# Start of a grouped-attention stage: six first pieces and four turned pairs in banks of their own, value tiles behind the first scores

## The chip, the cores and the metric

One core of a Trainium2 chip runs the whole program: a decoder of two layers on four sequences of 256 rows of 256 columns. The metric is the time on the device of one execution, in microseconds (us), as the median of the runs of a kernel.

## What is computed

The change lies in the attention of the last layer's block. Cut to what matters:

```python
h = rmsnorm(x, ln1_w)                       # B=4, S=256, H=256
q = rope((h @ Wq).reshape(B, S, 32, 128))   # 32 query heads of 128
k = rope((h @ Wk).reshape(B, S, 4, 128))    # 4 key heads, each for 8 query heads
v = (h @ Wv).reshape(B, S, 4, 128)
scores = einsum('bqhd,bkhd->bhqk', q, repeat(k, 8)) / sqrt(128)
scores = where(causal, scores, -1e9)
o = einsum('bhqk,bkhd->bqhd', softmax(scores), repeat(v, 8))
x = x + o.reshape(B, S, 32 * 128) @ Wo
```

Here x is the layer-normalised stream, which is normalised a second time for h. Everything is float32. Matmuls are made of three passes: each operand is split into a high part (fp32r) and a low part (the rest), and high by high, high by low and low by high are summed.

## The kernel before

The program is a row of six stages with a barrier between them. The stage in question is `stage_attention_1`; an expert stage (`stage_moe_1`) follows it. Each engine has a list of instructions that is written out in the order of the code, and waits on counting semaphores (`wait_ge`). Nothing else sets the order.

The stage has 64 steps (N = NP * B: 16 pairs of query heads by 4 sequences). A step takes one pair of heads of one sequence: `scores` (12 matmuls into a bank that already holds the causal mask), `maxima` on VectorE, `exps` on ScalarE, `normalise_probs` on GpSimd, `turn_probs` two steps later, `values` three steps later, `project` four steps later, and `residual`, which adds the result to the stream. Beside that each step makes one **piece**: a query or key head for two sequences, as six matmuls of 512 columns (`piece`). VectorE multiplies it by cosine and sine in three operations (`rotate`, L2229 to L2232, into prod), GpSimd adds the two products (`add`, L1889, into raw), ScalarE takes the high part (`high`, L2106) and GpSimd the low part (`low`, L1894).

PSUM has eight banks of 512 float32 columns: LONG (0 and 1) and SHORT (2) for scores, TURN0 and TURN1 (3, 4) for turned probabilities, PIECE (5), AV (6), OUT (7). ScalarE writes the causal mask into LONG and SHORT before scores are added to them (`mask_long` L2111, `mask_short` L2117).

Ahead of step 0 there is a start of the stage's own. VectorE normalises eight tiles (`normalise`), TensorE turns them in four pairs (`turn`, L1951) in banks 0 and 1 by turns, so that pair 2 waits until the low part of pair 0 is taken out of bank 0 (`h_high` L2094 on ScalarE, `h_low` L2216 on VectorE). Then come the six first pieces (key head 0 and the two query heads of pair 0, in two halves each), in banks PIECE and SHORT by turns, each waiting until the rotation of the piece two before it has read its bank. The eight value tiles (`values_of`, six matmuls of 512 columns each, `v_high` L2099, `v_low` L2261) stand between the pieces. TensorE waits for the last of them (s_vl) before step 0, and ScalarE for the same before the first mask. VectorE makes the residual's eight tiles (`residual_of`, L2209) before the first maxima.

```python
            for b in range(B):
                residual_of(b)
            e.wait_ge(s_res, NT)
            for n in range(N + PO + 1):
```

Of the kernel before, what the change touches and what calls it, by code (L numbers as in the profile page):

```python
# [13 lines left out]
B = 4  # L14
# [1742 lines left out]
def stage_attention_1(core, d):  # L1757
# [28 lines left out]
    with ExitStack() as ctx:  # L1786
# [45 lines left out]
        @block.sync  # L1832
        def _(e):
            e.dma_start(ln1[:], d["ln1"]).then_inc(s_ln1, 16)
            e.dma_start(wk[:], d["a1_wk"]).then_inc(s_wk, 16)
            e.dma_start(wv[:], d["a1_wv"]).then_inc(s_wv, 16)
            e.dma_start(wq[:, 0], d["a1_wq"][0:2].rearrange("h p k c -> p h k c")).then_inc(s_wq[0], 16)
            e.dma_start(rot[:], d["rot"]).then_inc(s_rot, 16)
            e.dma_start(seed[:], d["a1_seed"]).then_inc(s_seed, 16)
            e.dma_start(wo[:, 0], d["a1_wo"][:, 0:2, :]).then_inc(s_wo[0], 16)  # L1840
            e.dma_start(wq[:, 1], d["a1_wq"][2:4].rearrange("h p k c -> p h k c")).then_inc(s_wq[1], 16)
            e.dma_start(wo[:, 1], d["a1_wo"][:, 2:4, :]).then_inc(s_wo[1], 16)
            for p in range(2, NP + 2):
                if p < NP:
                    e.wait_ge(s_pc, number["q", p - 2, 1, 1] + 1)
                    e.dma_start(wq[:, p % 2], d["a1_wq"][2 * p:2 * p + 2].rearrange("h p k c -> p h k c"))\
                        .then_inc(s_wq[p % 2], 16)
                r = p - 2
                if r >= 2:
                    e.wait_ge(s_out, B * (r - 1))  # L1850
                    e.dma_start(wo[:, r % 2], d["a1_wo"][:, 2 * r:2 * r + 2, :]).then_inc(s_wo[r % 2], 16)

        V_BANKS = (TURN0, TURN1, AV, OUT, *LONG, AV, OUT)

        def bank_of(i):

            return ps[:, SHORT if i < FIRST and i % 2 else PIECE, :]

# [46 lines left out]
        def _(e):  # L1905
# [3 lines left out]
            const_low(e, 1)  # L1909
            for i in range(FIRST):  # L1910
                add(e, i)
                low(e, i)
            wo_low(e, 0)
            wq_low(e, 1)
            for n in range(N + 1):
# [15 lines left out]
        def _(e):  # L1931
# [12 lines left out]
            def turn(b):  # L1944
                e.wait_ge(s_n, 2 * b + 2)
                if b >= 2:
                    e.wait_ge(s_hl, b - 1)
                bank = ps[:, b % 2, :].rearrange("p (k t) -> p k t", k=KD)
                for j in range(2):
# [5 lines left out]
            def piece(i):  # L1955
                what = pieces[i]
                half = what[2]
                if i >= FIRST:
                    e.wait_ge(s_rp, 3 * i)
                elif i >= 2:  # L1960
                    e.wait_ge(s_rp, 3 * (i - 1))
                if i < FIRST:
# [40 lines left out]
            def turn_probs(s):  # L2003
                e.wait_ge(s_nrm, 2 * s + 2)
                if s >= 1:
                    e.wait_ge(s_tl, 2 * s)
# [10 lines left out]
            def values(s):  # L2017
                p, b = s // B, s % B
                g = p // 4
                e.wait_ge(s_tl, 2 * s + 2)  # L2020
                if s >= 1:
                    e.wait_ge(s_ol, s)
# [29 lines left out]
            piece(3)  # L2052
            piece(4)
            for t in range(4, 6):
                values_of(t)
            piece(5)
            for t in range(6, 8):
                values_of(t)
# [17 lines left out]
        def _(e):  # L2076
# [13 lines left out]
            def h_high(b):  # L2090
                e.wait_ge(s_tn, b + 1)
                bank = ps[:, b % 2, :].rearrange("p (k t) -> p k t", k=KD)
# [61 lines left out]
            wq_high(0)  # L2154
            h_high(2)
            const_high(1)
            h_high(3)
# [7 lines left out]
            for t in range(4, 6):  # L2165
                v_high(t)
            high(5)
            for t in range(6, 8):
                v_high(t)
            e.wait_ge(s_seed, 16)  # L2170
            e.wait_ge(s_vl, NT)
            mask_long(0)
            e.wait_ge(s_rp, 3 * FIRST)
            mask_short(0)
            wo_high(0)
            wq_high(1)
            for n in range(N + LV):
                for i in of_step.get(n - 1, ()):
                    high(i)
                if n + 1 < N:  # L2180
                    mask_long(n + 1)
                if n < N:
                    exps(n)
                if 0 <= n - LT < N:
                    turned_high(n - LT)
                if n + 1 < N:
                    mask_short(n + 1)
# [9 lines left out]
        def _(e):  # L2197
# [14 lines left out]
            def h_low(b):  # L2212
                e.wait_ge(s_hh, b + 1)
                bank = ps[:, b % 2, :].rearrange("p (k t) -> p k t", k=KD)
                for k in range(KD):
# [53 lines left out]
            def residual(s):  # L2269
                b = s % B  # L2270
                e.wait_ge(s_out, s + 1)
                e.tensor_tensor(res[:, 2 * b:2 * b + 2, :], res[:, 2 * b:2 * b + 2, :],  # L2272
                                ps[:, OUT, :].rearrange("p (t n) -> p t n", t=2), ALU.add).then_inc(s_add, 1)
# [11 lines left out]
            const_low(e, 0)  # L2285
            h_low(1)
            h_low(2)
# [9 lines left out]
            for t in range(4, 6):  # L2297
                v_low(t)
            rotate(5)
            for t in range(6, 8):  # L2300
                v_low(t)
            for b in range(B):
                residual_of(b)
            e.wait_ge(s_res, NT)
            for n in range(N + PO + 1):
# [4 lines left out]
                if n < N:  # L2310
                    maxima(n)
                if 0 <= n - PO - 1 < N:
# [458 lines left out]
```

## Time and profile before

| | us |
|---|---|
| median of 3 runs (1447.58 to 1452.32) | 1449.29 |
| the profiled execution | 1451.44 |
| its span | 1449.7 |
| TensorE (PE) busy in the span | 1267.7 (87%) |
| VectorE (DVE) | 958.6 (66%) |
| ScalarE (ACT) | 748.3 (52%) |
| GpSimd (POOL) | 632.2 (44%) |
| mean granted clock of TensorE | 0.938 of 2.4 GHz |

The busy shares are means over six stages. The grouped-attention stage begins at about 692 us of the span and ends at about 1140; the chain of work that ended last is, behind it, nearly all TensorE in the expert stage. What bounds the stage's start is read from the stretches of that start, not from the shares above.

### The profile page before, as it was taken

Reading aid. Unit: us, or ns where it says so; the run is one execution under the profiler, and the core shown is the slowest. Engines: PE = TensorE matmul, PEld = TensorE weight load, DVE = VectorE, ACT = ScalarE, POOL = GpSimd, SP = SyncE. Lnnn points to the kernel's source line nnn. Section 1 sums busy time; section 2 is a strip of 40 time slices with the busy share of each in tenths; the row PEclk is TensorE's granted clock in tenths of the full one; section 3 lists DMA queues with packets and bytes.
Section 4 is the critical chain, followed back from the end, with each engine's and each line's share of the span. In section 5 each row is a group of like instructions: output and inputs, shape, how many; then the busy total and the mean of one; then the engine's idle time right before and its main releaser. Section 6 shows DMA issues by size and latency. Waiting matters only on the chain. (4 is left out here: it accounts for less than half of the span.)

```text
span 1449.7 us, 23461 instructions
## 1 busy us (share of the span) xinstructions
PE 1267.7 (87%) x8399; PEld 995.9 (69%) x8399; DVE 958.6 (66%) x1761; ACT 748.3 (52%) x1685; POOL 632.2 (44%) x617
## 2 busy tenths in 40 slices
PE   5788668989889668888769999999999899999998
PEld 4665444744468444543558898898899778888887
DVE  5773773658745678883568898898898743344343
ACT  2555113346442136666357777786887444444442
POOL 5210101001044541200457887877886545555553
PEclk8999787989999869998879999999999899999999
DMA  2000400030000100000200010000100123323321
GB/s 75 1 2 2 117 3 0 1 111 0 0 1 1 40 1 2 2 2 1 82 8 16 16 30 16 30 16 16 30 16 16 46 98 109 119 101 111 117 101 55
DMA packets 28803, 54.80 MB, mean 38 GB/s; under 512 B 6170, under 2 KB 15706, under 8 KB 28612
## 3 DMA queue, kind: packets, MB, share of 16 engines
q1 hardware_dynamic: 28708, 53.55, 11.5%
q8 instruction: 58, 0.95, 0.3%
q14 instruction: 37, 0.30, 0.1%
HBM read 52.22 MB, written 1.21 MB: 37 GB/s over the span
## 5 line engine op out<-in xcount | busy, mean ns | idle before, releaser
L2618 DVE TENSOR_TENSOR e_act<-e_gated,ps 128x512 f32<-128x512 f32 x66 | 45.4, 688 | 157.5 <-POOL e_gated L2419 157.5
L1889 POOL TENSOR_TENSOR a_raw<-a_prod 128x512 f32<-128x512 f32 x72 | 93.0, 1291 | 65.6 <-DVE a_prod L2232 64.5
L2131 ACT ACTIVATE a_prob<-ps,a_nmax 128x128 f32<-128x128 f32 (+1 forms) x256 | 103.3, 413 | 7.0 <-DVE a_nmax L2239 6.2
L2419 POOL TENSOR_TENSOR e_gated<-e_gate,e_wb 128x512 f32<-128x512 f32 x66 | 85.1, 1291 | 49.4 <-ACT e_gate L2540 43.8
L2410 POOL TENSOR_TENSOR e_we_low<-e_we,e_we_high 128x768 fp32r<-128x768 f32 x33 | 61.3, 1856 | 86.9 <-ACT e_we_high L2545 86.2
L1665 DVE SCALAR_TENSOR_TENSOR m_acc<-ps,m_conv_w,m_acc 128x1020 f32<-128x1020 f32 (+2 forms) x60 | 76.1, 1275 | 28.5 <-ACT m_acc L1581 27.1
L1939 PE MATMUL ps<-a_k_high,a_q_high 128*128 128x128 f32 (+1 forms) x256 | 73.8, 288 | 20.0 <-ACT ps L2117 20.0
L1415 PE MATMUL ps<-m_ln_T,m_win 128*128 128x512 f32 x192 | 86.4, 604 | 3.6 <-DMA m_win<-in_m_winT 3.0
L612 DVE TENSOR_REDUCE x_nmax<-ps 128x2 bf16<-128x512 f32 x128 | 82.3, 689 | 10.0 <-PE ps L383 10.0
L2540 ACT ACTIVATE e_gate<-ps 128x512 f32<-128x512 f32 x66 | 39.3, 597 | 91.3 <-PE ps L2473 91.2
L518 ACT ACTIVATE x_probT<-ps 128x512 f32<-128x512 f32 x128 | 69.3, 595 | 31.0 <-PE ps L399 29.6
L1894 POOL TENSOR_TENSOR a_q_low<-a_raw,a_q_high 128x512 fp32r<-128x512 f32 x64 | 82.4, 1288 | 3.0 <-ACT a_q_high L2106 3.0
L95 POOL TENSOR_SCALAR row_var<-row_moments 128x2 f32<-128x2 f32 x20 | 4.9, 246 | 167.9 <-DVE row_moments L76 167.9
L2106 ACT ACTIVATE a_q_high<-a_raw 128x512 fp32r<-128x512 f32 x64 | 40.6, 635 | 71.3 <-POOL a_raw L1889 71.3
L2550 ACT ACTIVATE e_act_high<-e_act 128x512 fp32r<-128x512 f32 x66 | 41.5, 630 | 61.0 <-DVE e_act L2618 61.0
L1939 PE MATMUL ps<-a_k_low,a_q_high 128*128 128x128 f32 (+1 forms) x256 | 72.5, 283 | 0.0
L1939 PE MATMUL ps<-a_wo_high,a_o_high 128*128 128x256 f32 x256 | 71.7, 280 | 0.9 <-DVE res L2272 0.9
L2491 PE MATMUL ps<-e_we_high,e_act_low 128*128 128x256 f32 x256 | 72.4, 283 | 0.0
L2491 PE MATMUL ps<-e_we_low,e_act_high 128*128 128x256 f32 x256 | 72.4, 283 | 0.0
L1939 PE MATMUL ps<-a_k_high,a_q_low 128*128 128x128 f32 (+1 forms) x256 | 72.3, 282 | 0.0
L2491 PE MATMUL ps<-e_we_high,e_act_high 128*128 128x256 f32 x256 | 72.3, 282 | 0.0
L1939 PE MATMUL ps<-a_wo_high,a_o_low 128*128 128x256 f32 x256 | 71.7, 280 | 0.0
(429 smaller groups left out, 4302.1 us busy)
## 6 DMA issues: line engine op xcount, KB each, us to landing
e_wb<-token_weights SPq DMA_DIRECT2D x32, 512.0 KB, 4.0
e_we<-in_experts SPq DMA_DIRECT2D x33, 384.0 KB, 3.1
a_wq<-in_a_wq SPq DMA_DIRECT2D x16, 256.0 KB, 2.8
a_wo<-in_a_wo SPq DMA_DIRECT2D x16, 256.0 KB, 2.7
m_win<-in_m_winT SPq DMA_DIRECT2D x2, 1024.0 KB, 8.8
nf_pickU<-in_nf_pickU SPq DMA_DIRECT2D x1, 1152.0 KB
nf_raw<-in_ffn_w SPq DMA_DIRECT2D x3, 352.0 KB
x<-in_x SPq DMA_DIRECT2D x4, 256.0 KB, 6.1
```

Source lines behind the costliest of these rows:

```text
L518: e.activation(probT[:, n % 8, :], shifted_bank(n), ACT.Exp).then_inc(s_ex, 1)
L612: e.tensor_reduce(nmax[:, c % 2, :, col], score_bank(n).rearrange("p (j k) -> p j k", j=2), AX.X, ALU.max, negate=True).then_inc(s_nm, 1)
L1415: mm = e.matmul(ps[:, 2 * (i % RING) + half, :], win[:, k, at:at + P], lnT[:, k, half * BANK:(half + 1) * BANK], start=(k == 0), stop=(k = ...
L1665: e.scalar_tensor_tensor(sums[:, :, back:S], chan[:, :, 0:S - back], conv_w[:, c, TAPS - 1 - back:TAPS - back], sums[:, :, back:S], ALU.mu ...
L1889: e.tensor_tensor(raw[:, i % 2, :], prod[:, i % 2, 0, :], prod[:, i % 2, 1, :], ALU.add).then_inc(s_raw, 1)
L1894: e.tensor_tensor(low_part, raw[:, i % 2, :], high_part.bitcast(F32), ALU.subtract).then_inc(s_xl, 1)
L1939: mm = e.matmul(out, a, b, start=first and at == 0, stop=last and at == n - 1, skip_group_check=seeded and not first)
L2131: ins = e.activation(prob[:, n % PR, at + j * w:at + (j + 1) * w], bank[:, j * w:(j + 1) * w], ACT.Exp, bias=nmax[:, n % 2, j, t:t + 1], a ...
L2410: e.tensor_tensor(weL[:, slot, :], we[:, slot, :], weH[:, slot, :].bitcast(F32), ALU.subtract).then_inc(s_wl, 1)
L2419: e.tensor_tensor(gated[:, half, :], gate[:, half, :], wb[:, s % SLOTS, half * BANK:(half + 1) * BANK], ALU.mult).then_inc(s_gw, 1)
L2491: mm = e.matmul(ps[:, 4 + t // 2, t % 2 * D:(t % 2 + 1) * D], a[:, s % 2, t * P:(t + 1) * P], dw(w, s % SLOTS), start=(first and t % 2 == ...
L2618: e.tensor_tensor(act[:, half, :], gated[:, half, :], ps[:, 2 * half + 1, :], ALU.mult).then_inc(s_act, 1)
```

## The change

- The four turned pairs get a bank each (TURN0, TURN1, AV, OUT), and the six first pieces too (LONG twice, SHORT, PIECE, AV, OUT). The waits for a bank between them go.
- TensorE does the four turns, the six pieces, then step 0. Value tiles 0 to 2 stand behind the scores of step 0, 3 to 5 behind those of step 1, 6 and 7 behind those of step 2; `v_high` and `v_low` go with them.
- The low parts of the first three pieces go from GpSimd to VectorE, each one rotation behind. The rotation of the sixth piece stands behind the maxima of step 0.
- The masks of step 0 are written between the first high parts; in steps 0 to 3 the next short mask comes right behind the exps, and the high parts of new pieces behind it.
- The residual's tiles are made in steps 2 to 5, one pair in each. The first query weights are loaded ahead of the value weights.

```diff
             e.dma_start(wk[:], d["a1_wk"]).then_inc(s_wk, 16)
+            e.dma_start(wq[:, 0], d["a1_wq"][0:2].rearrange("h p k c -> p h k c")).then_inc(s_wq[0], 16)
             e.dma_start(wv[:], d["a1_wv"]).then_inc(s_wv, 16)
-            e.dma_start(wq[:, 0], d["a1_wq"][0:2].rearrange("h p k c -> p h k c")).then_inc(s_wq[0], 16)
...
-        V_BANKS = (TURN0, TURN1, AV, OUT, *LONG, AV, OUT)
+        V_BANKS = (TURN0, TURN1, AV, OUT) * 2
+        VALUES_AT = {0: (0, 1, 2), 1: (3, 4, 5), 2: (6, 7)}
+        FIRST_BANKS = (*LONG, SHORT, PIECE, AV, OUT)
+        turn_bank = lambda b: ps[:, (TURN0, TURN1, AV, OUT)[b], :].rearrange("p (k t) -> p k t", k=KD)
 
         def bank_of(i):
 
-            return ps[:, SHORT if i < FIRST and i % 2 else PIECE, :]
+            return ps[:, FIRST_BANKS[i] if i < FIRST else PIECE, :]
...
-            for i in range(FIRST):
+            for i in range(3):
+                add(e, i)
+            wq_low(e, 1)
+            e.wait_ge(s_xl, 3)
+            for i in range(3, FIRST):
                 add(e, i)
                 low(e, i)
             wo_low(e, 0)
-            wq_low(e, 1)
...
             def turn(b):
                 e.wait_ge(s_n, 2 * b + 2)
-                if b >= 2:
-                    e.wait_ge(s_hl, b - 1)
...
-                if i >= FIRST:
+                if i == FIRST:
+                    e.wait_ge(s_rp, 3 * (FIRST_BANKS.index(PIECE) + 1))
+                if i > FIRST:
                     e.wait_ge(s_rp, 3 * i)
-                elif i >= 2:
-                    e.wait_ge(s_rp, 3 * (i - 1))
...
                 if t == 0:
                     e.wait_ge(s_wcl, 2)
-                if t >= 6:
+                    e.wait_ge(s_hl, B)
+                if t in (2, 3):
+                    e.wait_ge(s_rp, 3 * (t + 3))
+                if t >= 4:
                     e.wait_ge(s_vl, t - 3)
...
-            turn(0)
-            turn(1)
-            turn(2)
-            piece(0)
-            turn(3)
-            piece(1)
-            piece(2)
-            for t in range(4):
-                values_of(t)
...
-            e.wait_ge(s_vl, NT)
+            for b in range(B):
+                turn(b)
+            for i in range(FIRST):
+                piece(i)
             for n in range(N + PO):
                 new = [*of_step.get(n, ())]
                 if n < N:
                     scores(n)
+                for t in VALUES_AT.get(n, ()):
+                    values_of(t)
...
+            e.wait_ge(s_seed, 16)
+            e.wait_ge(s_rp, 3)
+            mask_long(0)
             high(1)
+            wq_high(1)
             high(2)
-            for t in range(4):
-                v_high(t)
+            e.wait_ge(s_rp, 9)
+            mask_short(0)
             high(3)
             high(4)
...
-            e.wait_ge(s_vl, NT)
-            mask_long(0)
-            e.wait_ge(s_rp, 3 * FIRST)
-            mask_short(0)
-            wo_high(0)
-            wq_high(1)
             for n in range(N + LV):
-                for i in of_step.get(n - 1, ()):
-                    high(i)
+                if n > 3:
+                    for i in of_step.get(n - 1, ()):
+                        high(i)
...
                 if n < N:
                     exps(n)
+                if n <= 3:
+                    mask_short(n + 1)
+                for t in VALUES_AT.get(n, ()):
+                    v_high(t)
+                if n == 0:
+                    high(FIRST - 1)
+                    wo_high(0)
+                if n <= 3:
+                    for i in of_step.get(n - 1, ()):
+                        high(i)
...
             rotate(0)
-            h_low(3)
             rotate(1)
+            low(e, 0)
             rotate(2)
-            for t in range(4):
-                v_low(t)
+            low(e, 1)
             rotate(3)
+            low(e, 2)
             rotate(4)
...
-            for b in range(B):
-                residual_of(b)
-            e.wait_ge(s_res, NT)
...
                 if n < N:
                     maxima(n)
+                if n == 0:
+                    rotate(FIRST - 1)
+                if 0 <= n - 2 < B:
+                    residual_of(n - 2)
                 if 0 <= n - PO - 1 < N:
                     residual(n - PO - 1)
                 new = [*of_step.get(n, ())]
                 for i in new[:1]:
                     rotate(i)
+                for t in VALUES_AT.get(n, ()):
+                    v_low(t)
```

GpSimd's list at the start of the stage, before (a_raw is `add`, a_k_low and a_q_low are `low`):

```order
L1877 TENSOR_TENSOR a_wq_low<-a_wq,a_wq_high 128x512
L1873 TENSOR_TENSOR a_wv_low<-a_prob,a_wv_high 128x1024
L1889 TENSOR_TENSOR a_raw<-a_prod 128x512
L1894 TENSOR_TENSOR a_k_low<-a_raw,a_k_high 128x512
L1889 TENSOR_TENSOR a_raw<-a_prod 128x512
L1894 TENSOR_TENSOR a_q_low<-a_raw,a_q_high 128x512
```

and now:

```order
L1880 TENSOR_TENSOR a_wq_low<-a_wq,a_wq_high 128x512
L1876 TENSOR_TENSOR a_wv_low<-a_prob,a_wv_high 128x1024
L1892 TENSOR_TENSOR a_raw<-a_prod 128x512 x3
L1880 TENSOR_TENSOR a_wq_low<-a_wq,a_wq_high 128x512
L1892 TENSOR_TENSOR a_raw<-a_prod 128x512
L1897 TENSOR_TENSOR a_k_low<-a_raw,a_k_high 128x512
```

Three adds follow each other, their low parts are gone from this list, and the low part of the next query weights stands behind them.

VectorE's list around the first maxima, before (a_prod is `rotate`, a_v_low `v_low`, res `residual_of`, a_nmax `maxima`):

```order
L2229 TENSOR_TENSOR a_prod<-ps,a_rot 128x512
L2230 TENSOR_TENSOR a_prod<-ps,a_rot 64x512
L2232 TENSOR_TENSOR a_prod<-ps,a_rot 64x512
L2261 TENSOR_TENSOR a_v_low<-ps,a_v_high 128x512 x2
L2209 TENSOR_SCALAR res<-x,row_moments,row_rstd 128x256 x8
L2239 TENSOR_REDUCE a_nmax<-ps 128x2
L2242 TENSOR_REDUCE a_nmax<-ps 128x2
```

and now, from the third low part on:

```order
L1897 TENSOR_TENSOR a_q_low<-a_raw,a_q_high 128x512
L2234 TENSOR_TENSOR a_prod<-ps,a_rot 128x512
L2235 TENSOR_TENSOR a_prod<-ps,a_rot 64x512
L2237 TENSOR_TENSOR a_prod<-ps,a_rot 64x512
L2244 TENSOR_REDUCE a_nmax<-ps 128x2
L2247 TENSOR_REDUCE a_nmax<-ps 128x2
```

Low parts of pieces have come in between the rotations; the values' low parts and the residual's eight tiles no longer stand ahead of the first maxima.

ScalarE's list around the first exps, before (ps from a_seed is a mask, a_prob the exps):

```order
L2099 ACTIVATE a_v_high<-ps 128x512 x2
L2111 ACTIVATE ps<-a_seed 128x512
L2117 ACTIVATE ps<-a_seed 128x256
L2088 ACTIVATE a_wo_high<-a_wo 128x512
L2084 ACTIVATE a_wq_high<-a_wq 128x512
L2111 ACTIVATE ps<-a_seed 128x512
L2131 ACTIVATE a_prob,a_rsum<-ps,a_nmax 128x128 x2
```

and now, as a piece of the difference:

```order
+L2117 ACTIVATE ps<-a_seed 128x256
 L2106 ACTIVATE a_k_high<-a_raw 128x512
 L2106 ACTIVATE a_q_high<-a_raw 128x512
+L2111 ACTIVATE ps<-a_seed 128x512
+L2131 ACTIVATE a_prob,a_rsum<-ps,a_nmax 128x128 x2
+L2131 ACTIVATE a_prob,a_rsum<-ps,a_nmax 128x256 x2
+L2117 ACTIVATE ps<-a_seed 128x256
+L2099 ACTIVATE a_v_high<-ps 128x512 x3
```

The first exps stand behind the high parts of pieces 3 and 4, the short mask of step 1 right behind the exps, and the values' high parts behind that.

## Rows read from the trace of the kernel before

**Rows 1.** Windows: busy us (instructions) by engine, granted clock, DMA share, GB/s.
```profile
723.00:733.00 10.00, 0.33 (x2) 0.21 (x2) 5.88 (x12) 4.43 (x9) 4.15 (x4) 0.73 0.00 0
733.00:758.30 25.30, 19.70 (x90) 16.36 (x91) 17.06 (x30) 14.82 (x51) 16.22 (x16) 0.77 0.04 10
758.30:770.20 11.90, 11.89 (x85) 11.00 (x86) 10.79 (x21) 9.73 (x30) 8.98 (x9) 1.00 0.01 3
770.20:830.00 59.80, 56.32 (x384) 50.66 (x383) 51.84 (x95) 42.81 (x132) 47.33 (x45) 1.00 0.06 19
```

**Rows 2.** Timeline of TensorE: start, us, instruction; first score matmul of steps 0-6.
```profile
732.82 0.45 PE L1939 MATMUL ps<-a_k_high,a_q_high 128*128 128x128 f32 x1 [9.67 <-ACT ps L2117]
...
738.87 0.30 PE L1939 MATMUL ps<-a_k_high,a_q_high 128*128 128x128 f32 x1 [0.27 <-ACT ps L2117]
...
745.34 0.45 PE L1939 MATMUL ps<-a_k_high,a_q_high 128*128 128x128 f32 x1 [2.87 <-ACT ps L2117]
...
752.99 0.30 PE L1939 MATMUL ps<-a_k_high,a_q_high 128*128 128x128 f32 x1 [1.10 <-ACT ps L2117]
...
758.31 0.30 PE L1939 MATMUL ps<-a_k_high,a_q_high 128*128 128x128 f32 x1 [0.59 <-ACT ps L2117]
...
764.29 0.22 PE L1939 MATMUL ps<-a_k_high,a_q_high 128*128 128x128 f32 x1
...
770.19 0.22 PE L1939 MATMUL ps<-a_k_high,a_q_high 128*128 128x128 f32 x1
```

**Rows 3.** Timeline of TensorE: the first piece, and matmuls of 512 columns following each other.
```profile
699.92 0.79 PE L1939 MATMUL ps<-a_h_high,a_wk_high 128*128 128x512 f32 x1 [0.74 <-DVE a_h_low L2216]
...
708.46 0.39 PE L1939 MATMUL ps<-a_wv_high,a_h_low 128*128 128x512 f32 x1
708.69 0.39 PE L1939 MATMUL ps<-a_wv_high,a_h_high 128*128 128x512 f32 x1
...
736.74 0.63 PE L1939 MATMUL ps<-a_h_low,a_wq_high 128*128 128x512 f32 x1
737.17 0.63 PE L1939 MATMUL ps<-a_h_high,a_wq_low 128*128 128x512 f32 x1
...
759.77 0.40 PE L1939 MATMUL ps<-a_h_high,a_wq_high 128*128 128x512 f32 x1
```

**Rows 4.** Timeline of ScalarE, VectorE and GpSimd around the first piece.
```profile
698.29 0.63 ACT L2084 ACTIVATE a_wq_high<-a_wq 128x512 fp32r<-128x512 f32 x1 [0.21 <-DMA a_wq<-in_a_wq]
...
702.95 0.69 DVE L2229 TENSOR_TENSOR a_prod<-ps,a_rot 128x512 f32<-128x512 f32 x1 [1.99 <-PE ps L1939]
...
705.16 1.30 POOL L1889 TENSOR_TENSOR a_raw<-a_prod 128x512 f32<-128x512 f32 x1 [1.64 <-DVE a_prod L2232]
...
706.50 0.63 ACT L2106 ACTIVATE a_k_high<-a_raw 128x512 fp32r<-128x512 f32 x1 [1.93 <-POOL a_raw L1889]
```

**Rows 5.** Three lines of the code: count, min/median/max ns, first and last start.
```profile
L2574 DVE TENSOR_TENSOR e_t_low<-e_tT,e_t_high x4: 678/1216/5036, 1149.4 to 1157.2; 128x512 fp32r<-128x512 f32 x4
...
L2424 POOL TENSOR_TENSOR x<-x,res x1: 5002/5002/5002, 1151.7 to 1151.7; 128x2048 f32<-128x2048 f32 x1
...
L2209 DVE TENSOR_SCALAR res<-x,row_moments,row_rstd x8: 407/412/1375, 731.6 to 734.8; 128x256 f32<-128x256 f32 x8
```

**Rows 6.** Timeline of VectorE: value tiles, residual tiles, and the maxima of step 1.
```profile
714.20 2.49 DVE L2261 TENSOR_TENSOR a_v_low<-ps,a_v_high 128x512 fp32r<-128x512 f32 x4 [4.01 <-ACT a_v_high L2099]
...
731.59 4.59 DVE L2209 TENSOR_SCALAR res<-x,row_moments,row_rstd 128x256 f32<-128x256 f32 x8
...
740.89 0.39 DVE L2239 TENSOR_REDUCE a_nmax<-ps 128x2 f32<-128x256 f32 x1
741.21 0.68 DVE L2242 TENSOR_REDUCE a_nmax<-ps 128x2 f32<-128x512 f32 x1
```

**Rows 7.** Timeline of ScalarE in step 1: long mask, then (behind the exps) short mask.
```profile
742.71 0.58 ACT L2111 ACTIVATE ps<-a_seed 128x512 f32<-128x512 bf16 x1
...
744.80 0.39 ACT L2117 ACTIVATE ps<-a_seed 128x256 f32<-128x256 bf16 x1
```

More of the change, by code:

```diff
@@ L1945, in turn @@
                 e.wait_ge(s_n, 2 * b + 2)
-                if b >= 2:
-                    e.wait_ge(s_hl, b - 1)
-                bank = ps[:, b % 2, :].rearrange("p (k t) -> p k t", k=KD)
+                bank = turn_bank(b)
                 for j in range(2):
@@ L2004, in turn_probs @@
                 e.wait_ge(s_nrm, 2 * s + 2)
+                if s == 0:
+                    e.wait_ge(s_vl, 6)
                 if s >= 1:
@@ L2020, in values @@
                 e.wait_ge(s_tl, 2 * s + 2)
+                if s == 0:
+                    e.wait_ge(s_vl, NT)
                 if s >= 1:
@@ L2041, in project @@
                 mm.then_inc(s_out, 1)
-            turn(0)
-            turn(1)
-            turn(2)
-            piece(0)
-            turn(3)
-            piece(1)
-            piece(2)
-            for t in range(4):
-                values_of(t)
[L2052 to L2058, printed above, removed]
-            e.wait_ge(s_vl, NT)
+            for b in range(B):
+                turn(b)
+            for i in range(FIRST):
+                piece(i)
             for n in range(N + PO):
@@ L2091, in h_high @@
                 e.wait_ge(s_tn, b + 1)
-                bank = ps[:, b % 2, :].rearrange("p (k t) -> p k t", k=KD)
+                bank = turn_bank(b)
                 for k in range(KD):
@@ L2155, in _ @@
             h_high(2)
+            h_high(3)
             const_high(1)
-            h_high(3)
             high(0)
+            e.wait_ge(s_seed, 16)
+            e.wait_ge(s_rp, 3)
+            mask_long(0)
             high(1)
+            wq_high(1)
             high(2)
-            for t in range(4):
-                v_high(t)
+            e.wait_ge(s_rp, 9)
+            mask_short(0)
             high(3)
             high(4)
[L2165 to L2170, printed above, removed]
-            e.wait_ge(s_vl, NT)
-            mask_long(0)
-            e.wait_ge(s_rp, 3 * FIRST)
-            mask_short(0)
-            wo_high(0)
-            wq_high(1)
-            for n in range(N + LV):
-                for i in of_step.get(n - 1, ()):
-                    high(i)
+            for n in range(N + LV):
+                if n > 3:
+                    for i in of_step.get(n - 1, ()):
+                        high(i)
+                if n == 0:
+                    e.wait_ge(s_rp, 6)
                 if n + 1 < N:
@@ L2183, in _ @@
                     exps(n)
+                if n <= 3:
[8 more added lines that the diff above has]
+                        high(i)
                 if 0 <= n - LT < N:
                     turned_high(n - LT)
-                if n + 1 < N:
+                if 3 < n < N - 1:
                     mask_short(n + 1)
@@ L2213, in h_low @@
                 e.wait_ge(s_hh, b + 1)
-                bank = ps[:, b % 2, :].rearrange("p (k t) -> p k t", k=KD)
+                bank = turn_bank(b)
                 for k in range(KD):
@@ L2271, in residual @@
                 e.wait_ge(s_out, s + 1)
+                if s < B:
+                    e.wait_ge(s_res, 2 * b + 2)
                 e.tensor_tensor(res[:, 2 * b:2 * b + 2, :], res[:, 2 * b:2 * b + 2, :],
@@ L2285, in _ @@
             const_low(e, 0)
-            h_low(1)
-            h_low(2)
+            for b in range(1, B):
+                h_low(b)
             e.wait_ge(s_rot, 16)
             rotate(0)
-            h_low(3)
             rotate(1)
+            low(e, 0)
             rotate(2)
-            for t in range(4):
-                v_low(t)
+            low(e, 1)
             rotate(3)
+            low(e, 2)
             rotate(4)
[L2297 to L2301, printed above, removed]
-            for b in range(B):
-                residual_of(b)
-            e.wait_ge(s_res, NT)
             for n in range(N + PO + 1):
@@ L2311, in _ @@
                     maxima(n)
+                if n == 0:
+                    rotate(FIRST - 1)
+                if 0 <= n - 2 < B:
+                    residual_of(n - 2)
                 if 0 <= n - PO - 1 < N:
```

## The prediction

> **What bounds the kernel now.** I read the windows view first, cut at the places where TensorE's work changes character in the grouped-attention stage [rows 1]. From 758.30 us on TensorE is busy in 11.89 of 11.90 us, and in 56.32 of the 59.80 us after that: the steps of the stage run at TensorE's pace, some 6 us each. Before that they do not. From 723 to 733 us TensorE works 0.33 us in 10, and from 733 to 758.30 it is granted 0.77 of its clock. So the time that this change can reach lies between 700 and about 770 us, and whatever is won there moves all that follows to an earlier place, since what follows does not wait for a transfer.
>
> Next the timeline, for the first score matmul of steps 0 to 6 [rows 2]. They start at 732.82, 738.87, 745.34, 752.99, 758.31, 764.29 and 770.19 us. Step 0 began after TensorE had sat idle for 9.67 us, released by ScalarE's short mask; step 2 after 2.87 us. The reader is to see that step 0, and not the matmuls, is late. ScalarE writes the masks behind all eight value tiles, these wait for VectorE, and VectorE does them between the six first rotations and before the eight tiles of the residual.
>
> A matmul of 512 columns follows the next one by 0.23 us at the full clock (2.4 GHz) and by 0.43 us at the lower one (1.2 GHz) [rows 3]. Six of them, a piece or a value tile, are thus 1.38 or 2.56 us. The 12 score matmuls of step 4 took 1.46 us (758.31 to the piece at 759.77) [rows 2, 3]; at the lower clock I put them at 2.5, a little under twice that, an estimate.
>
> **Up to the first scores, part by part.** The first piece starts at 699.92 us [rows 3]; what it waits for (the low part of pair 1, the key weights) keeps its place. With a bank for every turned pair, pairs 2 and 3 are turned earlier, beside the wait for that low part: nothing on the path. The transfer of wq, now ahead of wv, can give ScalarE back the 0.21 us that it waited for wq [rows 4], or nothing; the value weights land that much later, and their turn on ScalarE is later too, behind pair 3. I take zero.
>
> The six pieces no longer wait for a rotation to empty a bank. Two of them run in part at the lower clock, and all are done by about 710 us. VectorE sets the pace instead. A rotation takes from 702.95 us to 705.16, when GpSimd starts adding its products [rows 4]: 2.15 us of VectorE and the signal. VectorE now does rotation 0, rotation 1, low 0, rotation 2, low 1, rotation 3, low 2 and then scores may start. A low part from two SBUF tiles is new on VectorE here; the same operation takes 678 ns at its shortest elsewhere, with 0.62 us from one pass to the next [rows 5, 6]. Four rotations are 8.6, three lows 1.95: 702.95 + 10.55 = 713.5 us. The add (1.30 us), the high part (0.63) and the hand-over of a piece end 2.0 us behind its rotation [rows 4], so they hide beside the next rotation; the short mask follows the high part of piece 2, at 712.5.
>
> One thing does not hide: while GpSimd runs an operation, VectorE's operation on two SBUF tiles stands still. In the expert stage that same low part took up to 5036 ns, in the very stretch in which GpSimd's 128x2048 addition took 5002 ns from 1151.7 on [rows 5]. Here every low starts when GpSimd is given an add. Where VectorE is first, GpSimd is what waits, 0.6 us; then low 2 meets GpSimd's low part of the next query weights and ends 0.4 us later, which I take. Where GpSimd is always first, each of two lows waits an operation of 1.3 us: 2.6 us more, my other end. Step 0 starts at 714.0 us where it was 732.82: **18.8 us earlier**.
>
> The Trainium skill ("SBUF — State Buffer", section "Who interferes with whom") says this as a rule against the change: an instruction of VectorE with two SBUF inputs and a GpSimd instruction that reads SBUF take turns, the second waiting for the whole of the first. By that rule the sum is the same, and its bad end is the rival on the port below; the trace agrees, with its 5036 ns.
>
> **What comes back in steps 0 to 6.** The value tiles are not gone: 11 us of TensorE (8 x 1.38) and their passes move into steps 0 to 2, the residual (4.59 us for eight tiles [rows 6]) into steps 2 to 5, rotation 5 into step 0. I follow the path from step to step.
>
> Step 0: TensorE was idle for some 4 us before it, and behind the idle 2.87 us in the rows it ran at the lower clock; so scores 2.5 us, first value tile 2.56, two more 2.76, piece 1.4: step 1 at 723.3. ScalarE must have the short mask back by then. Its exps stand behind high 4, which waits for two adds and a low on GpSimd (3 x 1.3 us) and a high part (0.7) from low 2 on: 718.6, high 0.6; long mask and exps 2.1 (742.71 to 744.80 [rows 7]); short mask 0.4: 721.7, in time.
>
> Step 1: scores, three value tiles, a piece, 7 us: step 2 at 730.2. VectorE's rotation of piece 6, three low parts of values (0.62 each [rows 6]) and maxima (0.39 and 0.68 us [rows 6]) with exps and mask behind them end at the same time.
>
> From here on VectorE, then exps and mask, end last. Step 2: rotation 2.15, three value lows 1.9, inverse and maxima 1.15, from 730.3 on, then 1.4 for the rest of exps and mask: step 3 at 737.0. Step 3: the first residual pair 1.15, rotation 2.15, two value lows 1.3, two passes on the turned probabilities 1.05, maxima 1.15: step 4 at 743.7. Step 4: residual pair, rotation, turned probabilities, a low of the output 0.65, maxima, and on ScalarE the turned high parts (0.85) between exps and mask: step 5 at 751.0. Step 5: the same, and project 1 waits for the first addition to the residual (0.65) and takes 1.4: step 6 at 757.9. Before, it was 770.19: **12.3 us earlier**. VectorE has next to no slack in these steps; that is where 6.5 of the 18.8 us go.
>
> The residual pairs are priced at their mean of the old place, 1.15 us. One tile is 412 ns in the middle and 1375 ns where GpSimd was at work [rows 5]. In the new place GpSimd is always at work: it normalises probabilities from the inverse on, which stands 1 us ahead of the pair. I take 1.5 us for a pair, between 0.7 (two free tiles) and 2.7 (two blocked): 4 x 0.35 = 1.4 us off. Sum: 12.3 - 1.4 = **11 us**, rounded.
>
> The profiled execution took 1451.44 us, its span 1449.7; the sum makes it 1440.4. The median of the runs shown, 1449.29, lies 2.15 below that execution, so I forecast **1438.3 us**. The measurement tells about 0.3% (4.35 us) from no change: faster means below 1444.9, slower above 1453.6.
>
> **The rivals.**
> *The clock stays up and the port is free.* The wait ahead of step 0 is some 4 us, not 9.67; if the clock holds through it, scores and first value tile lose no time, but step 1 then waits for ScalarE's short mask at 721.7: 1.6 us. With residual pairs at 0.7 another 3.2 us. 11 + 4.8: 1433.5 us. Against it: the clock did fall behind 2.87 us [rows 2].
>
> *The port goes GpSimd's way every time.* 2.6 us ahead of step 0, and 4 x (2.7 - 1.5) = 4.8 us in the residual pairs: 11 - 7.4 = 3.6, 1445.7 us, no change by the bound. For it stand the 5036 and 1375 ns [rows 5]; against it, that VectorE reaches low 0 and low 1 straight from the rotation whose end GpSimd has to be told of.
>
> *Half the clock through steps 0 to 6.* Slower than before. From scores 0 to scores 6 TensorE has some 37 us of work at full clock (6 scores 8.7, 8 value tiles 11, 6 pieces 8.4, four turns 2.8, three value products 3.3, two projections 2.8); the forecast lets it take 44. If the waits between its blocks keep the clock at the lower level, as it was granted 0.73 and 0.77 from 723 to 758 us [rows 1], the work takes 74 and step 6 starts at 788, 18 us later than before: 1467 us. It decides against the change once some 24 us of that work, beyond what I have at half clock, run so. Against it: after step 0 no wait in my path is over 1 us, and the value tiles fill the gaps that the old steps 0 to 2 had.
>
> **How the numbers follow.** Forecast 0.67: the order of the engines is written out, and every term has its row, but the chain has four engines in it. Clock up and port free 0.16. Port against it 0.12. Half clock 0.05. Faster by over 0.3%: 0.67 + 0.16 = 0.83. Within 0.3%: 0.12. Slower: 0.05. The forecast's own terms (lows 0 to 2.6, pairs 0.7 to 2.7, the clock 1.6) make it 1434 to 1443; the range reaches down to the first rival and up to near the second, **1432 to 1445 us**, and leaves out the half clock and the end of the port case.
>
> **What the new profile would show.** The first score matmul near 714 us after an idle of 3 to 5 us, that of step 6 near 758. Three k_low and q_low on VectorE of about 0.69 us, or 1.3 to 2 where blocked. Residual tiles of VectorE in pairs, one of each pair well over 412 ns. TensorE at 0.5 of its clock for some 5 us from 714 on, then at 1.0. From about 760 us on the same pace as before. I would be wrong if step 0 started after 718, if step 4 came later than 748, if the clock fell again in steps 1 to 5, or if steps 7 to 63 took longer than they did.

## The result, and the profile after

The changed kernel takes 1440.30 us (median of 6 runs, 1434.53 to 1442.71), and the kernel before, on the same chip, 1450.76 (6 runs, 1446.52 to 1454.79). The ratio is 0.9928, with a 95% interval of 0.9901 to 0.9956: **faster by 10.5 us**. The forecast was 11 us, to 1438.3 us, in a range of 1432 to 1445.

| | before | changed |
|---|---|---|
| the profiled execution | 1451.44 | 1438.6 |
| its span | 1449.7 | 1436.6 |
| first normalise of the stage | 692.23 | 689.37 |
| first piece | 699.92 | 697.06 |
| mean granted clock | 0.938 | 0.942 |

The spans differ by 13.1 us. Of these, 2.86 lie ahead of the stage, where the program is the same, and are no part of the change; all steps below are therefore counted from the first matmul of the first piece. The timeline of TensorE in the changed kernel (start in us, duration, instruction; in brackets the idle time before it and what ended it) has in this order the first piece, the first score matmuls of steps 0 to 4, and the first projection:

```profile
697.06 0.79 PE L1945 MATMUL ps<-a_h_high,a_wk_high 128*128 128x512 f32 x1 [1.59 <-DVE a_h_low L2221]
...
710.84 0.33 PE L1945 MATMUL ps<-a_k_high,a_q_high 128*128 128x128 f32 x1 [3.51 <-DVE a_q_low L1897]
...
719.36 0.22 PE L1945 MATMUL ps<-a_k_high,a_q_high 128*128 128x128 f32 x1
...
726.67 0.22 PE L1945 MATMUL ps<-a_k_high,a_q_high 128*128 128x128 f32 x1
...
733.55 0.30 PE L1945 MATMUL ps<-a_k_high,a_q_high 128*128 128x128 f32 x1
...
740.11 0.30 PE L1945 MATMUL ps<-a_k_high,a_q_high 128*128 128x128 f32 x1 [0.60 <-ACT ps L2117]
...
754.09 0.35 PE L1945 MATMUL ps<-a_wo_high,a_o_high 128*128 128x256 f32 x1 [2.18 <-DVE res L2279]
```

These answer to [rows 2]. The reader is to see that the 9.67 us of idle time ahead of step 0 are 3.51, ended by the last of VectorE's new low parts, and that there is a new wait of 2.18 us for VectorE ahead of the first projection. From the first piece on, in us:

| step | before | forecast | changed | gain | second profile of the changed kernel |
|---|---|---|---|---|---|
| 0 | 32.90 | 14.1 | 13.78 | 19.1 | 13.86 |
| 1 | 38.95 | 23.4 | 22.30 | 16.7 | 22.39 |
| 2 | 45.42 | 30.3 | 29.61 | 15.8 | 29.72 |
| 3 | 53.07 | 37.1 | 36.49 | 16.6 | 36.60 |
| 4 | 58.39 | 43.8 | 43.05 | 15.3 | 43.16 |
| 5 | 64.37 | 51.1 | 50.05 | 14.3 | 50.17 |
| 6 | 70.27 | 58.0 | 58.53 | 11.7 | 58.66 |
| 7 | 77.56 | | 67.37 | 10.2 | 65.95 |
| 10 | 97.75 | | 87.57 | 10.2 | 86.16 |

(The forecast column is without its 1.4 us for the residual, which no step was given.) From step 7 to step 63 the gain stays between 10.14 and 10.24 us; the steady step is 5.90 us in both. The last column, from the run further down, shows that step 6 to 7 differs between executions of the same kernel.

The windows of the changed kernel, columns as in [rows 1], show at what the first steps run:

```profile
700.00:714.00 14.00, 10.49 (x44) 8.73 (x44) 13.22 (x20) 3.81 (x7) 9.11 (x7) 0.87 0.07 21
714.00:722.00 8.00, 8.00 (x41) 6.65 (x40) 4.51 (x8) 6.05 (x17) 5.39 (x6) 0.96 0.00 0
722.00:730.00 8.00, 7.61 (x39) 6.02 (x38) 5.63 (x11) 5.01 (x15) 5.78 (x6) 1.00 0.00 0
730.00:738.00 8.00, 7.12 (x40) 5.59 (x40) 7.91 (x17) 4.79 (x16) 5.25 (x6) 1.00 0.00 0
738.00:746.00 8.00, 7.40 (x51) 6.49 (x49) 7.91 (x14) 6.59 (x24) 7.59 (x8) 1.00 0.10 35
746.00:758.00 12.00, 9.17 (x58) 8.34 (x58) 11.81 (x21) 6.92 (x21) 5.96 (x7) 0.90 0.00 1
```

VectorE (third count) is busy 13.22 of the 14 us around the start of step 0 (710.84), and from its first rotation at 700.09 to the end of the last low part at 710.79 it has no wait: it sets the pace there, as forecast. From 714 to 730 (the rest of step 0, step 1 and half of step 2) TensorE is busy 15.61 of 16 us and VectorE is free for 5.9. From 730 to 758 it is the other way round: VectorE 27.63 of 28 us, TensorE with gaps. VectorE's own lines tell why:

```profile
704.42 0.69 DVE L1897 TENSOR_TENSOR a_k_low<-a_raw,a_k_high 128x512 fp32r<-128x512 f32 x1
...
707.19 0.69 DVE L1897 TENSOR_TENSOR a_q_low<-a_raw,a_q_high 128x512 fp32r<-128x512 f32 x1
...
709.96 0.83 DVE L1897 TENSOR_TENSOR a_q_low<-a_raw,a_q_high 128x512 fp32r<-128x512 f32 x1
...
719.55 0.69 DVE L2234 TENSOR_TENSOR a_prod<-ps,a_rot 128x512 f32<-128x512 f32 x1 [3.34 <-PE ps L1945]
...
726.88 0.69 DVE L2234 TENSOR_TENSOR a_prod<-ps,a_rot 128x512 f32<-128x512 f32 x1 [2.28 <-PE ps L1945]
...
731.83 1.34 DVE L2214 TENSOR_SCALAR res<-x,row_moments,row_rstd 128x256 f32<-128x256 f32 x2
...
738.37 1.17 DVE L2214 TENSOR_SCALAR res<-x,row_moments,row_rstd 128x256 f32<-128x256 f32 x2
...
744.14 2.32 DVE L2214 TENSOR_SCALAR res<-x,row_moments,row_rstd 128x256 f32<-128x256 f32 x2
...
751.06 2.29 DVE L2214 TENSOR_SCALAR res<-x,row_moments,row_rstd 128x256 f32<-128x256 f32 x2
```

Three low parts (0.69, 0.69, 0.83 us), then waits of 3.34 and 2.28 us for pieces 6 and 7 in steps 0 and 1, and only behind these waits, where VectorE has no time left, the four residual pairs.

### The profile page after: what moved, and what is told of

It reads as the page before. It is cut to its first block and busy times, and to the rows that moved or that the text cites. A ratio compares the mean times of both kernels' runs of the same rounds, so it can differ in the third digit from the quotient of the medians.

```text
span 1436.6 us, 23466 instructions
## 1 busy us (share of the span) xinstructions
PE 1263.4 (88%) x8399; PEld 993.2 (69%) x8399; DVE 961.5 (67%) x1764; ACT 747.1 (52%) x1685; POOL 629.6 (44%) x614
## 3 DMA queue, kind: packets, MB, share of 16 engines
q1 hardware_dynamic: 28708, 53.55, 11.6%
```

## The experiments

Most were run once, and single times of one kernel differ by several us (the kernel before, on the second of these chips, 1442.10 to 1456.91). They are judged by their steps, counted from the first piece, and the time is given beside that of the kernel before on the same chip. Two parts of the change were never undone: the banks of the six pieces, and the place of the value tiles as a whole. What these are worth is read from the rows of the two kernels, not shown by an experiment.

**The residual pairs.** Theory: pairs in steps 2 to 5 stand on the path, and VectorE's waits in steps 0 and 1 could hold them. Rival: their place does not matter.

```diff
-                if 0 <= n - 2 < B:
-                    residual_of(n - 2)
+                if n < 2:
+                    residual_of(2 * n)
+                    residual_of(2 * n + 1)
```

> The residual's pairs are made in steps 0 and 1 (two pairs each, behind the maxima and ahead of the rotation), where VectorE waited 3.34 and 2.28 us for TensorE, instead of steps 2 to 5. Places are told from the first matmul of the first piece; the changed kernel has step 0 at 13.78, step 4 at 43.05, step 6 at 58.53, step 10 at 87.57 us. Theory (the pairs, stretched by GpSimd to 7.1 us, are what gives back the gain between steps 3 and 8): step 4 at 41, step 6 at 54, step 10 at 81 to 83 us. Rival (TensorE's value tiles and ScalarE's exps and masks set those steps, VectorE only follows): step 10 at 87 us or later.

Measured: 1430.83 us (before: 1444.95). The steps start at 13.79, 22.35, 29.67, 36.54, 42.86, 49.86, 55.85, and step 10 at 83.36: steps 0 to 5 stand within 0.2 us of the changed kernel, step 6 is 2.7 us earlier. VectorE's timeline, residual pairs 0 to 3 and the first operation of rotations 6, 7 and 8:

```profile
714.12 3.34 DVE L2214 TENSOR_SCALAR res<-x,row_moments,row_rstd 128x256 f32<-128x256 f32 x4
717.77 0.69 DVE L2234 TENSOR_TENSOR a_prod<-ps,a_rot 128x512 f32<-128x512 f32 x1 [0.30 <-PE ps L1945]
...
722.72 2.21 DVE L2214 TENSOR_SCALAR res<-x,row_moments,row_rstd 128x256 f32<-128x256 f32 x4
...
725.09 0.69 DVE L2234 TENSOR_TENSOR a_prod<-ps,a_rot 128x512 f32<-128x512 f32 x1 [0.16 <-PE ps L1945]
...
731.05 0.69 DVE L2234 TENSOR_TENSOR a_prod<-ps,a_rot 128x512 f32<-128x512 f32 x1 [0.92 <-PE ps L1945]
```

The waits of 3.34 and 2.28 us took in 5.55 us of residual. What follows: 2.7 us is the whole effect of the four pairs up to step 6, and 2.5 of it lie in step 5 (8.48 us in the changed kernel, 5.99 here). There pair 3 (2.29 us) stood right ahead of the addition that the first projection waits for, and the wait of 2.18 us is gone. Pairs 0 to 2 moved next to nothing by step 5: with pair 0 gone, VectorE waits 0.92 us for piece 8 instead, and from 735 to 745 us GpSimd is busy 10.00 of 10 us. The theory holds for step 5 only: it had step 4 at 41 and step 10 at 81 to 83 us. Of the 4.2 us at step 10, 1.4 are the clock in step 6 (below).

**All pairs ahead of the maxima**, where they stood before the change. Theory: the first steps lose 1 to 2 us, since the first exps waited for a high part anyway, and the later steps win 6. Rival: the place of the pairs does not matter, and the first steps lose 2 to 4 us.

```diff
             rotate(4)
+            for b in range(B):
+                residual_of(b)
...
-                if 0 <= n - 2 < B:
-                    residual_of(n - 2)
```

> All four residual pairs stand ahead of the first maxima, as in the kernel before; the rest as changed. Theory: the first maxima come some 4 us later, of which exps 0 hid 2 us (they waited for the high part of piece 4 until 716.0 us), so step 1 starts 1 to 2 us later than 22.30 us; steps 3 to 7 lose their pairs and win 6 us: step 10 at 83 to 84 us. Rival (the place of the residual doesn't matter, or it was right to move it): step 10 at 87.57 us plus the 2 to 4 us that the first steps lose, 89 to 91 us.

Measured: 1444.37 us (before: 1444.95); step 1 at 24.15 (+1.85), step 2 at 32.67 (+3.06), step 6 at 58.83, step 10 at 86.33. The eight tiles took 5.74 us in a row. The first maxima came 5.7 us later, the first exps 2.6. Behind a wait of 1.63 us for the short mask ahead of step 1 the clock fell (0.50 from 730 to 733 us), and step 1 to 2 took 8.52 us instead of 7.31. Step 1 is the theory's; step 10 lies between the two expectations, and against the changed kernel's second profile (86.16) it neither wins nor loses. Putting the pairs late was therefore no gain over putting them early; only the gaps of steps 0 and 1, used pair by pair, are.

**The first low parts back on GpSimd.** Theory: three GpSimd passes of 1.3 us beside three adds set step 0. Rival: a low part is as dear on VectorE, because of the port.

```diff
             for i in range(3):
                 add(e, i)
+                low(e, i)
             wq_low(e, 1)
-            e.wait_ge(s_xl, 3)
...
             rotate(1)
-            low(e, 0)
...
```

> The first three low parts are on GpSimd again, each behind its add; the rest as changed. Theory (moving them to VectorE took GpSimd's 3.3 us per piece off the path, and the port cost only what GpSimd waited): step 0 at 15 to 15.5 us instead of 13.78, step 10 at 87.5 to 89 us. Rival (the port makes a low part on VectorE as dear as on GpSimd): step 0 at 13.8 us or earlier, step 10 at 87 us or earlier.

Measured: 1438.48 us (before: 1444.95); step 0 at 15.12 (+1.34), step 1 at 24.91 (+2.61), step 10 at 88.67, which is 2.5 later than the second profile of the changed kernel. Step 0 to 1 took 9.79 us instead of 8.52: TensorE had waited 4.71 us and had half the clock until 718 us, 6 us into step 0, not some 3.7. The theory holds, and the move of the low parts is 1.3 of the 19.1 us at step 0.

**Value tiles ahead of step 0.** Theory: two value tiles fill the idle 3.51 us and keep the clock up in step 0, but steps 2 to 7 are set by VectorE and ScalarE. Rival: TensorE's lost time is carried through, and every step comes 2.3 to 2.8 us earlier.

```diff
             for i in range(FIRST):
                 piece(i)
+            values_of(0)
+            values_of(1)
...
                 for t in VALUES_AT.get(n, ()):
-                    values_of(t)
+                    if t > 1:
+                        values_of(t)
```

> TensorE makes value tiles 0 and 1 ahead of the scores of step 0, in the 3.51 us in which it was idle. Theory (VectorE and ScalarE set steps 2 to 7, the clock and TensorE only steps 0 and 1): no lower clock in step 0, step 1 up to 0.9 us earlier than 22.30 (the short mask is there 0.9 us ahead of it), steps 2 and 3 up to 2 us earlier, step 10 at 86 to 87.6 us. Rival (TensorE's lost time is carried through): every step from 1 on, and step 10, 2.3 to 2.8 us earlier, 85 us.

Measured: 1443.37 us (before: 1444.95); step 1 at 21.63 (0.67 earlier), but step 2 at 31.45 (1.84 later) and step 10 at 87.92. TensorE's timeline of this kernel, first score matmuls of steps 0 and 1:

```profile
715.00 0.33 PE L1945 MATMUL ps<-a_k_high,a_q_high 128*128 128x128 f32 x1 [0.81 <-DVE a_q_low L1897]
...
722.81 0.45 PE L1945 MATMUL ps<-a_k_high,a_q_high 128*128 128x128 f32 x1 [2.75 <-ACT ps L2120]
```

The windows of the same kernel around step 1 (granted clock third from the end):

```profile
719.00:723.00 4.00, 1.25 (x6) 0.78 (x5) 3.12 (x5) 3.37 (x12) 3.09 (x3) 0.90 0.00 0
723.00:727.00 4.00, 4.00 (x16) 3.71 (x17) 2.97 (x6) 3.93 (x13) 2.25 (x2) 0.50 0.00 0
```

The idle time ahead of step 0 is 0.81 us, but the work taken from step 0 left 2.75 us of waiting for the short mask ahead of step 1, and there the clock fell to 0.50. The idle time had only moved one step on. Neither expectation had this: step 1 is the theory's, but steps 2 and 3 came 1.84 us later, where the theory had them up to 2 us earlier, and step 10 lies beyond both. One tile ahead, on top of the first experiment, gave little:

> As the run with the residual in the idle time of steps 0 and 1, and TensorE makes one value tile, not two, ahead of the scores of step 0: 1.4 of its 3.15 us of idle are filled. Theory (the clock falls in the wait that is left, be it ahead of step 0 or of step 1, which waits for its short mask at about 21.4 us): if a wait of 2 us lets it fall, step 2 at 30 us or later and step 10 at 83.4 to 85; if it stays up, step 1 at 21.4, step 2 at 28.7, step 10 at 82.5 to 83.4 us.

Measured: 1435.43 us (before: 1448.38); step 1 at 21.71, step 10 at 83.08 against 83.36 in the first experiment: 0.3 us. TensorE waited 1.84 us ahead of step 0 and 0.43 ahead of step 1, and the clock fell behind the first (0.50 from 714.5 to 717.5 us). Even so step 2 came at 29.41 and step 10 at 83.08, earlier than expected for a clock that falls.

**ScalarE's order.** In steps 0 to 3 the change puts the next mask straight behind the exps, and the high parts of new pieces behind it. Theory: this order lets VectorE and TensorE of the next step go on. Rival: ScalarE has the time either way.

```diff
-                if n > 3:
-                    for i in of_step.get(n - 1, ()):
-                        high(i)
+                for i in of_step.get(n - 1, ()):
+                    high(i)
...
-                if n <= 3:
-                    mask_short(n + 1)
...
-                if 3 < n < N - 1:
+                if n < N - 1:
                     mask_short(n + 1)
```

> ScalarE's order in steps 0 to 3 is again that of the later steps: high parts of new pieces ahead of the exps, the next short mask behind the turned probabilities (and so behind the values' high parts too); the rest as changed. Places from the first matmul of the first piece, as before; the changed kernel has step 1 at 22.30, step 10 at 87.57 us. Theory (the short mask releases steps 1 to 3, so its place next to the exps is a part of the gain): the mask of step 1 moves behind three value high parts, a high part and the output weights, 2.6 us, of which 0.9 is slack: step 1 at 24 us, step 10 at 89 to 91 us. Rival (TensorE's own work sets steps 1 to 3): step 10 at 87.6 to 88 us.

Measured: 1443.97 us (before: 1448.38); step 1 at 24.24 (+1.9), step 3 at 41.37 (+4.9), step 5 at 55.08 and step 6 at 64.30, which are 4.9 and 5.6 later than in the changed kernel's second profile, and step 10 at 92.79. TensorE waited 1.54 us for the short mask ahead of step 1 and 1.81 ahead of step 3:

```profile
721.46 0.30 PE L1945 MATMUL ps<-a_k_high,a_q_high 128*128 128x128 f32 x1 [1.54 <-ACT ps L2117]
...
738.59 0.30 PE L1945 MATMUL ps<-a_k_high,a_q_high 128*128 128x128 f32 x1 [1.81 <-ACT ps L2117]
```

The two waits are 3.35 of the 4.9 us, and 1.2 came with the half clock behind the first (step 1 to 2 took 8.49 us, not 7.31). Whether the clock falls there each time is not shown by one profile. What is lost behind step 5 is not counted to the order: there the clock fell behind a wait of 2.17 us for VectorE that the changed kernel has too, and behind this wait a fall comes in one execution and not in another (below). The theory holds, with more than it asked for (step 10 at 89 to 91 us): at 4.9 us this order is the largest part of the change among those that were undone.

**Banks and transfers.** The two old turn banks with their wait, and wv ahead of wq. Theory: these parts only move work that nothing waits for. Rival: they set the first piece.

```diff
+            e.dma_start(wv[:], d["a1_wv"]).then_inc(s_wv, 16)
             e.dma_start(wq[:, 0], d["a1_wq"][0:2].rearrange("h p k c -> p h k c")).then_inc(s_wq[0], 16)
-            e.dma_start(wv[:], d["a1_wv"]).then_inc(s_wv, 16)
...
-        turn_bank = lambda b: ps[:, (TURN0, TURN1, AV, OUT)[b], :].rearrange("p (k t) -> p k t", k=KD)
+        turn_bank = lambda b: ps[:, (TURN0, TURN1)[b % 2], :].rearrange("p (k t) -> p k t", k=KD)
...
+                if b >= 2:
+                    e.wait_ge(s_hl, b - 1)
```

> The turned pairs share two banks again, with their wait, and the value weights are loaded ahead of the first query weights; the rest as changed. Theory (both lie beside other work): the first piece starts as late behind the stage's first instruction as in the changed kernel, step 0 at 13.8 us, step 10 at 87.6 us, all within 0.3 us. Rival (pair 3's late low part holds up pieces 3 to 5, which now follow each other without a wait): step 0 up to 1 us later, step 10 up to 1 us later.

Measured: 1437.03 us (before: 1448.38). From the first piece on the steps are those of the changed kernel up to step 6 (13.76 to 58.53), but the first piece itself comes 8.53 us behind the stage's first normalise (688.35 to 696.88), not 7.69. All four turns stand ahead of it on TensorE, and with two banks the last two wait for low parts. TensorE in this kernel:

```profile
694.23 1.09 PE L1957 MATMUL ps<-ident,a_normed 128*128 128x128 f32 x4 [2.93 <-DVE a_h_low L2223]
696.15 1.09 PE L1957 MATMUL ps<-ident,a_normed 128*128 128x128 f32 x4 [0.83 <-DVE a_h_low L2223]
```

Both waits are for low parts, not for a transfer. So the banks are worth 0.84 us to this order, and "the first piece starts as late" missed; step 10 at 86.05 missed 87.6 too, for the reason that follows. In this kernel step 6 to 7 took 7.29 us where the changed kernel's profile had 8.84, with the same wait of 2.18 us ahead of the projection. The windows of the changed kernel around that wait:

```profile
751.00:755.00 4.00, 1.82 (x14) 1.55 (x12) 3.97 (x6) 3.74 (x14) 2.20 (x2) 1.00 0.01 2
755.00:759.00 4.00, 4.00 (x22) 3.81 (x21) 3.60 (x9) 1.62 (x5) 2.48 (x3) 0.57 0.00 0
```

The second of these windows in the kernel with the old banks:

```profile
755.00:759.00 4.00, 4.00 (x30) 3.69 (x30) 3.94 (x10) 1.78 (x7) 2.66 (x3) 1.00 0.00 0
```

Whether that came with the banks or differs from execution to execution was asked of the changed kernel itself, unedited:

> The changed kernel as it is, a second time. In its first profiled execution the clock fell in step 6, behind 2.18 us of idle TensorE, and step 6 to 7 took 8.84 us; with the two old turn banks the same idle cost nothing (7.29 us). Theory (the fall differs from execution to execution of one kernel): either 8.8 or 7.3 us from step 6 to 7 here, all other steps from the first piece on within 0.1 us of the first profile, step 10 at 87.6 or at 86.0 us behind the first piece. Rival (four banks and the earlier wq bring it about): 8.8 us again. Theory and rival agree if 8.8 comes; 7.3 decides for the theory. Median 0.7% below the kernel before.

Measured: 1439.33 us (before: 1448.85; 6 runs, 1433.21 to 1442.88; ratio 0.9935, 0.9909 to 0.9961). Step 6 to 7 took 7.29 us, steps 0 to 6 stood within 0.13 us of the first profile, and step 10 came at 86.16. The wait ahead of the projection was 2.18 us again, at 753.07, and the windows around it show no fall:

```profile
750.00:754.00 4.00, 1.82 (x14) 1.55 (x13) 3.97 (x6) 3.72 (x14) 2.18 (x2) 1.00 0.01 2
754.00:758.00 4.00, 4.00 (x32) 3.69 (x30) 3.94 (x9) 1.62 (x5) 2.52 (x3) 1.00 0.00 0
```

The fall in step 6 is a matter of the execution, not of the banks. Without it the stage gives 11.6 us, with it 10.2.

**A better version.** In the first experiment step 5 is late by ScalarE: in step 4, whose order is already the later one, the mask and exps stand behind a high part that waits for GpSimd (TensorE waits 0.88 us for the short mask ahead of step 5). ScalarE's timeline there:

```profile
741.14 0.63 ACT L2106 ACTIVATE a_q_high<-a_raw 128x512 fp32r<-128x512 f32 x1 [1.41 <-POOL a_raw L1892]
741.68 0.58 ACT L2111 ACTIVATE ps<-a_seed 128x512 f32<-128x512 bf16 x1
```

So the first experiment was run with ScalarE's first order kept through step 4 (3 becomes 4 in its four conditions).

> As the run with the residual in the idle time of steps 0 and 1 (step 4 at 42.86, step 5 at 49.86, step 10 at 83.36 us), and ScalarE keeps the order of the first steps (exps, short mask, then high parts) in step 4 too. Theory (with the pairs gone, step 5 waits 0.88 us for the short mask, whose exps stood behind a high part that waited for GpSimd): step 5 0.9 us earlier, step 10 at 82.4 to 82.7 us, and a time of 1435 us or 1.0% below the kernel before. Rival (VectorE or GpSimd end last there too): step 10 at 83.3 us; then 0.9% below.

Measured: 1432.85 us (before: 1448.38; 7 runs; ratio 0.9902, 0.9864 to 0.9939); step 5 at 48.92 (0.94 earlier than in the first experiment), step 10 at 82.69, 0.67 earlier. The theory holds. It was measured once more beside the changed kernel:

> The version with residual pairs in steps 0 and 1 and ScalarE's first-steps order through step 4, a second time, beside the changed kernel on the same chip. Theory (the stage's 4.9 us reach the end, as nothing behind the stage waits for a transfer): step 10 at 82.7 us behind the first piece, median 3.3 to 5 us below the changed kernel's. Rival (what is won in the stage is taken back behind it): within 1.5 us of the changed kernel's median.

Measured: 1435.09 us (before: 1448.85; 6 runs, 1430.93 to 1437.49; ratio 0.9913, 0.9891 to 0.9934), 4.24 us under the changed kernel's median on that chip; step 10 at 82.60, 3.56 earlier. The theory holds, and 3.56 us in the trace are less than its 4.9 because the changed kernel's clock did not fall this time. The single runs of the two overlap, so the times alone make it likely; the trace, where each step from 4 on is earlier in both profiles of this version, shows that the stage is shorter.

## Why the prediction was right

- **Step 0.** Forecast 18.8 us earlier, measured 19.1. Four rotations and three lows on VectorE, in a row from 700.09 to 710.79, set it. The port went as the forecast took it. GpSimd's timeline:

```profile
702.31 1.29 POOL L1892 TENSOR_TENSOR a_raw<-a_prod 128x512 f32<-128x512 f32 x1 [1.68 <-DVE a_prod L2237]
704.47 1.80 POOL L1892 TENSOR_TENSOR a_raw<-a_prod 128x512 f32<-128x512 f32 x1 [0.88 <-DVE a_prod L2237]
707.24 1.77 POOL L1892 TENSOR_TENSOR a_raw<-a_prod 128x512 f32<-128x512 f32 x1 [0.96 <-DVE a_prod L2237]
```

  A low starts on VectorE at 704.42 and 707.19, 0.05 us ahead of the add, and the add takes 1.80 and 1.77 us instead of 1.29: GpSimd paid 0.5 us each time (0.6 forecast). Low 2 met the query weights on GpSimd (708.97) and took 0.83 us, 0.14 more, where 0.4 was forecast. That one waits while the other is first is what the Trainium skill says ("SBUF — State Buffer", section "Who interferes with whom"); these rows agree, with 0.5 us of the low's 0.69. That GpSimd's additions were second is what kept the rival on the port away at step 0.
- **Clock behind step 0.** Forecast half clock for some 5 us; it was some 3.3 (711.23 to about 714.5). Step 0 to 1 so took 8.52 us instead of 9.3, and with step 0 itself 0.3 earlier this put step 1 at 22.30 instead of 23.4.
- **Steps 2 to 6.** Forecast 27.7 us from step 2 to step 6, and 1.4 for the residual: 29.1; measured 28.92. The total was right, and its parts were not, so that it came out even is in part luck: steps 2 to 4 took 20.4 us and step 5 8.5, where 20.8 and 6.9 were forecast and the 1.4 had no place. The term that was mis-sized is the residual. Forecast were four pairs of 1.5 us, all 6.0 on the path; they took 1.34, 1.17, 2.32 and 2.29, and taking all four away moved step 6 by 2.7 us only, nearly all of it in step 5 (first experiment). In step 4 the forecast had VectorE and the turned high parts on ScalarE, and not that ScalarE's mask and exps stand behind a high part that waits for GpSimd. With the pairs gone this is what makes step 5 late: letting mask and exps go first there moved it by 0.94 us. How much of the changed kernel's own steps 2 to 4 it sets beside VectorE was not separated.
- **The clock.** "If the clock fell again in steps 1 to 5" did not come; it fell at the start of step 6 (755.6 us) in one of two profiles, for 1.55 us. The forecast did not have this term: it held that "after step 0 no wait in my path is over 1 us", and the projection in step 5 waited 2.18. The rival of half clock through all steps did not come: from 722 to 746 us 1.00 was granted.
- **Steps 7 to 63** did not change, as forecast.
- **The sum**: 11 us forecast; 10.2 and 11.6 in the two profiles, 10.5 and 9.5 in the medians. The mechanism up to step 0 is the forecast one. That the sum is so close is in part luck: the fall of the clock in step 6 is worth 1.4 us, comes in one execution and not in another, and had no term. One sum of the forecast is off: with the lows' 2.6 us and the pairs' 4.8 its own terms reach 1445.7, not 1443 us.

## What to carry to other kernels

When an engine comes free earlier, look for the waits that this opens on it: work moved off the front belongs into those waits, not behind them, where the same engine sets the pace; here that was worth 2.7 us on top of the change's 10 to 12. In a queue that is served in order, put what the next step waits for (the mask) ahead of what waits for another engine (the high part): 4.9 us here. And idle time filled by moving work is not gone until one has looked at the step that the work came from.

## What was not expected of the hardware

The same wait of TensorE, 2.18 us in the same place of the same kernel, was followed by a granted clock of 0.57 in one execution and of 1.00 in another, and step 6 took 1.55 us longer in the first. So a single profile's price of such a gap can be nothing or all of it; two profiles of one kernel were needed to see it. In the six profiles of this case that have this wait, of 2.16 to 2.18 us, the clock fell behind it in two. Behind shorter waits it fell too: 1.54 and 1.81 us (the old order of ScalarE), 1.63 (all pairs ahead), 1.84 (one value tile ahead). The length of a wait alone therefore did not tell here; what did is not shown.
